# Linear attention in a macaron block: centred key-value sums, one product for numerators and denominators, shuffled queries, and a new order

## The reference

```python
x = x + 0.5 * ffn(layernorm(x))
x = x + attn(layernorm(x))
x = x + 0.5 * ffn(layernorm(x))

def attn(h):                          # 8 heads of 16
    q, k, v = heads(h @ Wq.T), heads(h @ Wk.T), heads(h @ Wv.T)
    q = q * cos + rotate_half(q) * sin
    k = k * cos + rotate_half(k) * sin
    kv, ksum, vsum = einsum('bshd,bshe->bhde', k, v), k.sum(axis=1), v.sum(axis=1)
    num = einsum('bshd,bhde->bshe', q, kv) * 16 ** -0.5 + vsum[:, None]
    den = einsum('bshd,bhd->bsh', q, ksum) * 16 ** -0.5 + 512
    o = num / den[..., None] + conv5(v, lepe_w, lepe_b)   # 5 taps, each feature alone
    return (o * (h @ Wg.T)) @ Wo.T

def ffn(h):                           # 8 experts, 128 -> 256 -> 128, and a shared one
    shared = (silu(h @ sg.T) * (h @ su.T)) @ sd.T
    scores, idx = top_k(sigmoid(h @ router_w.T + routing_bias), 2)
    routed = sum over both k of scores[k] / scores.sum() * expert[idx[k]](h)
    return shared + routed
```

## Time and profile before

| what | value |
|---|---|
| median of 3 runs | 480.28 us (478.69 to 480.45) |
| profiled execution, span | 501.9 us |
| TensorE busy in it | 462.0 us, 92%, 2975 instructions |
| VectorE busy | 346.8 us, 69% |
| GpSimd busy | 282.3 us, 56% |
| ScalarE busy | 271.0 us, 54% |
| mean DMA rate | 107 GB/s |

### The profile page before, as it was taken

One profiled execution on the slowest core, in us unless ns is written; L12 is line 12 of the kernel. 1 busy time (PEld: TensorE's weight loads), 2 busy tenths in 40 slices (PEclk: granted clock), 3 DMA queues, 4 the chain that ended last, 5 costly groups with the idle time before them and its releaser, 6 DMA issues.

```text
span 501.9 us, 9741 instructions
## 1 busy us (share of the span) xinstructions
PE 462.0 (92%) x2975; PEld 382.8 (76%) x2975; DVE 346.8 (69%) x1064; ACT 271.0 (54%) x612; POOL 282.3 (56%) x290
## 2 busy tenths in 40 slices
PE   8979899989899999899989998999998998999896
PEld 4868678877788787688767877877776777888776
DVE  4999993333568865868889898899876532454355
ACT  5936135555476555476546664655464555565421
POOL 4148556665567245566636655686654555666562
PEclk9999999999999999999989999999999999999999
DMA  8981233253421334321132322114342253543323
GB/s 237 370 283 39 68 107 116 80 167 113 111 73 64 101 80 116 92 68 57 54 102 56 91 75 74 43 39 123 88 128 84 78 163 105 150 113 104 86 73 106
DMA packets 74353, 53.68 MB, mean 107 GB/s; under 512 B 9664, under 2 KB 68928, under 8 KB 74304
## 3 DMA queue, kind: packets, MB, share of 16 engines
q1 hardware_dynamic: 66112, 36.26, 24.4%
q0 software_dynamic: 8192, 16.79, 11.0%
HBM read 26.87 MB, written 26.15 MB: 106 GB/s over the span
## 4 chain that ended last, share of the span: by engine, by line
PE 50%; DVE 26%; issue 10%; ACT 6%; another core or an unknown queue 5%; DMA 2%; POOL 0%; SPq 0%; DVEq 0%; ACTq 0%; POOLq 0%
PE pool L888 12%; PE pool L877 6%; PE gu L843 5%; PE gu L845 5%; PE gu L844 5%; DVE X L1242 3%; PE gu L804 2%; DVE hs L1219 2%; PE pool L826 2%; DVE hs L1223 2%; PE gu L802 2%; DVE raw L1421 2%; PE gu L803 2%; DVE stats L1253 2%
## 5 line engine op out<-in xcount | busy, mean ns | idle before, releaser
L1176 POOL DMA_INDIRECT yg<-y_sorted,places x128 | 124.2, 970 | 94.3 <-PE gu L845 42.0
L1156 POOL DMA_INDIRECT x_sorted<-xn,places x128 | 129.7, 1013 | 83.3 <-PE gu L845 30.8
L1219 DVE TENSOR_TENSOR hs<-gs,gu 128x512 f32<-128x512 f32 x92 | 60.7, 663 | 89.4 <-ACT gs L1033 64.7
L1033 ACT ACTIVATE gs<-gu 128x512 f32<-128x512 f32 x124 | 72.1, 583 | 70.8 <-PE gu L804 24.8
L888 PE MATMUL pool<-w,hT 128*128 x708 | 99.3, 283 | 11.6 <-ACT hT L1039 9.7
L888 PEld LDWEIGHTS pool<-w,hT 128*128 128x128 f32 x708 | 87.6, 191 | 26.4 <-issue 23.0
L843 PE MATMUL gu<-w,xbt_hi 128*128 x177 | 81.8, 462 | 1.8 <-DVE xbt_lo L1205 1.5
L1039 ACT ACTIVATE hT<-pool 128x512 f32<-128x512 f32 x92 | 53.3, 580 | 36.2 <-PE pool L877 24.8
L845 PE MATMUL gu<-w,xbt_hi 128*128 x177 | 70.0, 396 | 0.0
L844 PE MATMUL gu<-w,xbt_lo 128*128 x177 | 69.9, 395 | 0.0
L1014 ACT ACTIVATE ys<-pool 128x256 f32<-128x256 f32 x92 | 34.5, 376 | 62.6 <-PE pool L888 34.2
(11 more groups left out here) (132 smaller groups left out, 786.8 us busy)
## 6 DMA issues: line engine op xcount, KB each, us to landing
xb<-x_sorted SPq DMA_DIRECT2D x85, 128.0 KB
y_sorted<-ys SPq DMA_DIRECT2D x85, 128.0 KB
x_sorted<-yg SPq DMA_DIRECT2D x6, 512.0 KB, 6.3
X<-x_dram SPq DMA_DIRECT2D x8, 256.0 KB, 4.8
x_sorted<-xn,places POOLq DMA_INDIRECT x128
yg<-y_sorted,places POOLq DMA_INDIRECT x128
out_dram<-X SPq DMA_DIRECT2D x8, 256.0 KB
raw<-gate_w_dram SPq DMA_DIRECT2D x4, 256.0 KB, 4.8
```

Source lines behind the costliest of these rows:

```text
L1033: nc.scalar.activation(dst, src, ACT.Silu).then_inc(silu_done, 1)
L1156: nc.gpsimd.indirect_dma_start(x_sorted[g], bass.IndirectOffsetOnAxis(places[g][:, k, t:t + 1], 0), xn[:, b, t % T], None).then_inc(scatte ...
L1176: nc.gpsimd.indirect_dma_start(yg[slot][:, k, t], None, y_sorted[g], bass.IndirectOffsetOnAxis(places[g][:, k, at:at + 1], 0)).then_inc(ga ...
L1219: v.tensor_tensor(hs[n % HB][:].rearrange("p (j i) -> p j i", j=2)[:, 0:k], gs[n % GB][:].rearrange("p (j i) -> p j i", j=2)[:, 0:k], bank ...
```

## The change

**Queries and gate.** The permuted weight `wqp` is gone (`NA`, the number of 128-column attention weights, goes from 5 to 4). The units Q and VG become one unit, QG, with the queries in one half of the bank and the gate in the other; the sample's normalized rows are free after it. VectorE makes the swapped queries from the one product with an instruction that moves rows between partitions in blocks of 32 (`stream_shuffle`, L1402), into SBUF, and multiplies them there by the sine (L1410).

**Values.** Values by feature come from the values by token, by four transposes on TensorE (`v_turn`, L965), and `vT` is copied from there.

**Centred sums.** `centre` (VectorE) makes a diagonal matrix of minus the mean of the values and adds the mean to the convolution's bias. TensorE multiplies it by the block mask (L975, columns `MEAN` of the bank), ahead of the key-value product. `mask_kv` adds that times `ksum` to the masked sums. Thus the attention is computed as the mean of the values plus a correction whose numerators need no `vsum`.

**One product.** `kv_ks` holds the 128 columns of the masked sums beside the 8 of `ksum`. A unit ND on the `gu` banks multiplies each 128 tokens of `q_rot` by all 136 columns, token by feature. VectorE adds 512, inverts (as before, on 32 columns) and scales the numerators straight from PSUM in two operations of 128x256 (`scale`, L1491). TensorE transposes the result back (`att_turn`, L985), and VectorE adds the convolution (L1501) and multiplies by the gate (L1507), now two steps. Removed are ScalarE's widening and its copy of the spread reciprocals, TensorE's denominators, their transposes and the numerators, and VectorE's product with the spread reciprocals.

**Order.** The plan's length for loading expert numbers (`regs`) goes from 40 to 6, and every letter of `URGENCY` is new. `PACE` stays.

```diff
-NA = 5
+NA = 4
 URGENCY = (
-    "WLFWSb^ukX}PPPnPCcJNT;RELRIJR8=6@K?didXL<:VH0&UF>CSFKJaSYsKdP]JRNN5L3reTK/]YP[UOTFBVLWXSmQM{YMeWcIMPVu]/PKNPLU"
+    "cl#kdB-CPDjcb-r@eE-oSQ{Fw<s#BEdL)+@G#ITPo}jQH)J,p9Nx#ZrHx}N4,%GGYf<s;SW;AC}}#v5ZS=Vw]&q[4#uj&Gmie#>ij<E1bQF?+6"
...
-            op(("regs", r), "PE", 40, ("table", g), ("front", ("R", r - 1), 0) if r >= 1 else None)
+            op(("regs", r), "PE", 6, ("table", g), ("front", ("R", r - 1), 0) if r >= 1 else None)
...
+        op(("q_swap", b), "DVE", 62, ("front", qg, 1), last("q_add"), *(("cut_w_lo", e) for e in range(E)))
...
+        op(("v_turn", b), "PE", 45, ("v_tok", b))
...
+        op(("centre", b), "DVE", 30, ("vT", b), last("kv"), last("conv0"))
...
+        op(("conv0", b), "ACT", 72, ("centre", b), last("sum"))
...
+        op(("kv", b), "PE", 117, ("rope_add", b), ("v_tok", b), ("centre", b))
+        op(("mask", b), "DVE", 60, ("kv", b), ("front", ("A", b - 1, "ND"), 0) if b else None)
+        op(("front", nd, 1), "PE", 46, ("mask", b), ("q_add", b), ("front", ("A", b - 1, "ND"), 0) if b else None)
...
+        op(("invert", b), "DVE", 50, ("front", nd, 0), last("scale"))
+        op(("scale", b), "DVE", 74, ("invert", b), last("att_turn"))
+        op(("att_turn", b), "PE", 45, ("scale", b))
...
-            return {"Q": ((q_cos_done, b + 1), (q_sin_done, b + 1)), "VG": ((vT_done, b + 1), (og_done, b + 1)),
+            return {"QG": ((og_done, b + 1), (q_cos_done, b + 1)), "ND": ((scaled, b + 1), (scaled, b + 1)),
...
+                    if which == "ND":
+                        once.wait_ge(kv_ks_done, b + 1)
+                        once.wait_ge(q_rot_done, b + 1)
+                        for t in (2 * j, 2 * j + 1):
+                            mm = pe.matmul(dst[:, j, (t % 2) * ND:(t % 2 + 1) * ND], q_rot[:, t * P:(t + 1) * P], kv_ks[:],
+                                           start=True, stop=True)
...
             def kv(b):
...
                 once.wait_ge(k_rot_done, b + 1)
                 once.wait_ge(v_tok_done, b + 1)
+                once.wait_ge(centred, b + 1)
...
+                pe.matmul(pool_ps[m][:, MEAN], bmask[:], v_mean[:], start=True, stop=True)
                 for t in range(T):
                     mm = pe.matmul(pool_ps[m][:, 0:VW], k_rot[:, t, :], v_tok[:, t, :], start=t == 0, stop=t == T - 1)
...
+                v.stream_shuffle(qs, bank(u)[:, 1], swapped).then_inc(q_swapped, 1)
...
+                v.tensor_scalar(v_mean[:], ident, vsum[b % 2][:, 0:1], -1.0 / S, ALU.mult, ALU.mult)
+                v.tensor_scalar(conv_bias[:], vsum[b % 2][:], 1.0 / S, tap_bias[:, 0:1], ALU.mult,
+                                ALU.add).then_inc(centred, 1)
...
-                v.tensor_tensor(kv_bd[:], src[:, 0:D], bmask[:], ALU.mult)
-                v.tensor_scalar(ks_bd[:], hmask[:], src[:, D:D + 1], None, ALU.mult).then_inc(kv_bd_done, 1)
+                v.tensor_tensor(kv_ks[:, 0:D], src[:, 0:D], bmask[:], ALU.mult).then_inc(mask_link, 1)
+                v.tensor_scalar(kv_ks[:, D:], hmask[:], src[:, D:D + 1], None, ALU.mult)
+                once.wait_ge(mask_link, b + 1)
+                v.scalar_tensor_tensor(out=kv_ks[:, 0:D], in0=src[:, MEAN], scalar=src[:, D:D + 1], in1=kv_ks[:, 0:D],
+                                       op0=ALU.mult, op1=ALU.add).then_inc(kv_ks_done, 1)
...
+                v.tensor_tensor(att, misc("att_turn", b)[:], conv, ALU.add).then_inc(o_sum_done, 1)
```

## The result

The changed kernel takes 476.50 us (median of 4 runs, 475.78 to 476.58), the kernel before 479.58 beside it (478.69 to 480.45): a ratio of 0.9925, 95% interval 0.9903 to 0.9946. A second set gave 475.38 against 480.16, 0.9899 (0.9864 to 0.9933). By the medians the change saves 3.1 us in the first set and 4.8 in the second, where 8.3 were forecast. The time lies inside the range, and the direction was right; the size was not.

What follows compares the result with a forecast made beforehand. The prediction took TensorE's place in its own order as the program's clock, with the moves following. Terms 6.9 + 0.6 + 2 - 1 = 8.5 us brought the median from 480.28 to 471.8, said as 472; range 463 to 485.

Steps and rivals of the forecast that it cites:

- TensorE's saving in size: In the attention, replaced TensorE operations take 1.55 us less per sample, 12.4 us for eight.
- Where it falls: TensorE work sinks 1.8 us before pair 84, from 35.9 to 31.5 up to the last gate, 8.8 to 2.5 behind.
- what lies behind the last gathers' gate: At the program's end, some 6.3 us less TensorE work behind sample 7's sixth gather gate, worth only 0.6 us.
- The factor 1.14: Pairs 0 to 84: trace time 379.7 us over 332.8 of priced TensorE work; it multiplied the 1.8 us saved there.
- VectorE taken at 0: Net added VectorE work, at most 1.7 us a sample and 13 in all, costs 0, with ends at 0 and 4 us.
- the gap of 21.6 us: Profiled execution's 501.9 us against the median of 480.28, taken as idle time that profiling adds.
- first rival: VectorE becomes the bound: one hidden-product wait per sample passed to TensorE, 13.6 us, giving 485.4; chance 0.20.
- TensorE under 90% busy: Sign that VectorE became the bound: TensorE under 90% busy in the middle, with VectorE over 92%.
- the stretch at 91% that had cost nothing: From 289.0 to 335.6 us VectorE was busy 91% and TensorE 94%, read as VectorE costing TensorE nothing.
- The new waits, 1 us: In the attention, waits around values' transposes, centring, merged product and result's transposes cost 1 us in all.
- The order, 2 us: More TensorE work between pairs' last fronts and hidden transposes returns 0 to 9 us of waits; 2 taken.
- The second rival: TensorE was not the clock; moves and landings hold the end, saving turns idle, 479 to 480; chance 0.16.

Runs made afterwards that it cites:

- e10: Kernel before, with the shared units of samples 1 and 3 of the third sublayer, at its very end, reduced to a token: 478.54 us, ratio 0.9973.
- e14: Kernel before, with two more VectorE reads of the queries ahead of each sample's cosine product, 10 us in all: 492.58 us, ratio 1.0255.
- e13: Changed kernel, centring moved to ScalarE, shuffle and last mask operation cut to few columns, waits and order kept: 472.51 us, ratio 0.9837.
- e2: Kernel before, with query halves and gate half computed as one product instead of three, 11.3 us less TensorE: 480.36 us, ratio 1.0002.
- e11: Changed kernel, with TensorE's transposes of hidden rows earlier in its order in the first 24 pairs: 475.71 us, ratio 0.9908.
- e12: Changed kernel's operations put in the order of the kernel before, each new step in the old one's place: 496.67 us, ratio 1.0336.
- e7: Kernel before, with 11.3 us of TensorE's query and gate products and three of VectorE's four convolution taps cut: 477.82 us, ratio 0.9953.
- e9: Changed kernel, with the shared units of samples 1 and 3 of the third sublayer, there in the middle, reduced to a token: 476.89 us, ratio 0.9918.
- e3: Changed kernel, with each half of the query-and-gate unit computed twice, 11.3 us more TensorE: 484.67 us, ratio 1.0086.
- e5: Changed kernel, with three of VectorE's four convolution taps cut to 8 columns, 13 us less VectorE: 471.87 us, ratio 0.9815.

## Why the prediction was off, step by step

**TensorE's saving in size: close.** 1.55 us a sample were forecast. By the distances from start to start the removed and replaced steps took 48.9 us in the eight samples before (queries, values and gate 23.4, key-value sums 6.9, denominators 7.6, spread 4.0, numerators 7.0) and take 38.9 after (queries and gate 11.8, transposes of values 3.9, means and key-value sums 10.2, merged product 9.6, transposes back 3.4): 1.25 a sample, waits behind a step counted in. At the usual distances of the table, without such waits, it is 1.6.

**Where it falls: right.** Up to pair 84 the work sank by 1.3 us (1.8 forecast); from there to the end by 11.1 (10.7 forecast), which shortened the end by 4.8 us (5.4 forecast). That what lies behind the last gathers' gate is worth little agrees with e10: 9 us of TensorE there, 1.3 us of time, with an interval that includes none.

**The factor 1.14: a product of the disturbed trace.** In the undisturbed one pairs 0 to 84 hold 340.2 us of work in 358.0, a factor of 1.05 (1.08 with the forecast's own 332.8). This costs the forecast some 0.3 us.

**VectorE taken at 0: the step that failed.** Its added work was sized well for the middle: 1.7 us a sample were said (the terms given add up to 1.77); the rows above and those of the removed product give 0.74 + 0.84 + 0.49 + 0.35 - 0.75 = 1.67, and in pairs 30 to 66 VectorE's busy time rose by 13.9 us, where 14 were forecast. The shuffle takes 0.737 us (taken as 0.69). The estimate from the Trainium skill, "VectorE: DVE Perf Modes", section "The perf-mode tier table (the rule you actually need)", of 0.6 to 0.7 us is a little under the row.

What was wrong is the room that I gave it. The shares of the earlier trace rows come from a trace 4% longer than the times that I forecast from. In the second one the same pairs (30 to 66) take 191.4 us, VectorE is at 89%, and after the change at 94% (183.7 of 195.1). I had seen the gap of 21.6 us, put it down to profiling and took the gain off the median, but read the shares against the stretched windows. Scaled to the median, 185 of 197 us, 94%, would have been past the point at which my own first rival decides. Nor is a share of 89% room: in the kernel before 10 us more on VectorE cost 12.4 (e14), and half of its chain there runs through VectorE. In place of 0 the stretch from pair 24 to 56 lost 4.6 us. Taking the added work off again gives 3.9 of them back (e13), 3.0 at the same clock, and 2.9 of the whole time; the rest of the loss stays open.

The first rival named the right mechanism at the wrong price, 13.6 us. And the sign that I had named for it, TensorE under 90% busy, cannot show it: records of TensorE stretch over its waits (e2 above), and so the stretch at 91% that had cost nothing was judged by a measure that cannot tell.

**The new waits, 1 us: about right for those named, and one missing.** The waits that I named are small in the second stretch (TensorE before the merged product 0.5 us in all, before the transposes back 0.3). The one that counts, 1.84 us before a pair's front, I had not listed: the bank of the query unit, which now two operations of VectorE have to read.

**The order, 2 us: a right size by luck.** The rest fell by 2.3 us in pairs 0 to 24, but e11 shortens the distances again without giving it back. And the two waits that the term was taken from, 9.7 and 5.1 us in the first trace, were mostly the disturbance; in the second one they are

```profile
PE pool L877 <- DVE hs L1219: 3.5, 10, 1.0
PE pool L888 <- ACT hT L1039: 0.3, 1, 0.3
```

What took the idle time out of pairs 0 to 24 stays open. So does what the new order by itself would do for the old operations: e12 shows the reverse case only, and an order of the new kernel's kind for the old steps was not tried.

**The second rival**, that TensorE is not the clock, had the better evidence for the attention: e2, e7 and e9 take 9 to 11 us from TensorE and bring 0 to 1 us by that. The Trainium skill, "Trainium Kernel Development and Optimization", section Performance Expectations, calls matmul busy time a bad measure of how close a kernel is to its roofline; e2 fits that, with TensorE busy for 93% where it was 97%, in the same length. This rival fails at the two ends of the program, where the 9.5 us were won, and for added work (e3).

With about as much VectorE work cut as the change had brought (e13 cuts most of that work itself, e5 other work, the taps) the time is 472.5 and 471.9. That is the forecast, which had its VectorE term at 0; but the two runs leave out work that the kernel needs, and no complete version here does as well.

## What to carry to other kernels

Compare the span of the profiled execution with the median first; if it is some per cent longer, scale its windows before any engine's share is read as room, or profile again. In a program of fixed lists, room is not what a busy share leaves over: put some work on the engine, and take some off, at the place of the change. Here adding 10 us on VectorE cost 9 to 12 and 11 on TensorE cost 8, while taking as much off returned between nothing and 5. And compare the clock of two windows before their lengths.

## What else the runs showed

The granted clock of single runs moves the time more than I knew. In one set of 25 runs of the kernel before, the eight at a mean clock of 0.999 to 1.000 took 477.2 to 479.8 us, and the three at 0.989 took 481.1 to 483.6. One low stretch follows a gap of TensorE. Behind the gap of 1.84 us shown above (windows of the changed kernel, the third number from the end is the clock):

```profile
218.00:219.90 1.90, 0.06 (x2) 0.06 (x1) 1.67 (x6) 0.00 (x0) 1.88 (x2) 1.00 0.14 56
219.90:221.00 1.10, 1.10 (x5) 0.92 (x6) 0.67 (x3) 0.47 (x2) 0.91 (x2) 1.00 0.06 22
221.00:222.00 1.00, 1.00 (x5) 0.44 (x3) 1.00 (x3) 1.00 (x4) 0.72 (x1) 0.50 0.00 0
222.00:223.00 1.00, 1.00 (x6) 0.77 (x5) 1.00 (x4) 0.93 (x3) 0.97 (x1) 0.50 0.17 66
223.00:224.00 1.00, 1.00 (x6) 1.00 (x5) 0.63 (x2) 0.60 (x1) 0.69 (x2) 0.50 0.16 66
```

TensorE stands for 1.84 us, works again for a microsecond at full clock, and then has the lower of its two levels, 1.2 GHz, for some 3.4 more. The gap alone does not decide it: e11's trace has the same gap of 1.84 us and the full clock behind it. Still, an edit that takes work out of TensorE's list can pay part of it back: e2 and e9 ran at mean clocks of 0.985 to 0.996 and 0.984 to 0.995, where the kernels that they came from had 0.989 to 1.000 and 0.992 to 0.998.
